# Seven-product block multiplies (Strassen in Winograd's form) in place of eight, with all engine queues written out anew

## Chip, cores and metric

The kernel runs on one core of one Trainium2 chip. The metric is device time in microseconds (us). Before the change the median of 3 runs is 212.93 us (212.54 to 213.19).

## What is computed

```
q = cond @ Wq.T + bq                 # (2, 512), one query row for each batch
k = x @ Wk.T + bk ; v = x @ Wv.T + bv  # x is (2, 2048, 512)
scores = q . k / sqrt(32)            # for each of 16 heads
attn = clip(scores, 0, 1)
out = x + (attn * v) @ Wo.T + bo     # attn scales a head's 32 columns of v
```

All is float32. `k` is never formed: `Wk.T q` is folded once into a small matrix `a`, and the scores are `a . x`. Two large products are left, the values (4096 x 512 by 512 x 512) and the outputs (the same size).

## The kernel before

**Splitting.** A float32 operand is split into `hi`, a rounded copy (float32r), and `lo`, the rest. A product takes three passes: hi by hi, hi by lo, lo by hi (`product`, L208 to L210). The rounded copy is made by ScalarE (ACT), the difference `lo_part` (L424) by VectorE (DVE).

**Tiling.** x stands transposed in SBUF, features on partitions, in 8 chunks of 512 rows, batches in turn. A chunk's values are 4 output tiles by 4 contraction tiles by 3 passes, 48 matmuls of 128x128 weights by 512 columns, into four PSUM banks (`v_bank`); its outputs are 48 more (`o_bank`). With 8 matmuls for the scores (L222, L223) and one that spreads them over partitions (L235) a chunk is 105 matmuls.

**Order.** In `step` TensorE (PE) runs scores and values of chunk c, then the outputs of chunk c-1. DVE adds the bias and multiplies by the clipped scores (`context_tile`, L457), makes `lo`, and adds the output bank, the bias and x (`add_output`, L474). Loops over chunks (`Fori`) hold six of the eight chunks. The last output tile is done in two halves of 256 columns.

**Opening.** x and Wv of the first chunk come in four parts (`first_values`), mixed with the two small chains for `a`: `rows` with Wq (`q_rows`, L276, L279), back to DVE, `rows` with Wk (`a_rows`), back again. Nine bf16 matmuls on zeros (L285) stand ahead. DMAs for x, weights and stores are all issued by SyncE (SP). GpSimd (POOL) clears four tiles and copies `select`.

## Time and profile before

| | |
|---|---|
| median of 3 runs | 212.93 us |
| span of the profiled execution | 211.6 us |
| PE busy | 203.8 us (96%), 895 matmuls |
| DVE busy | 109.0 us (52%), 162 instructions |
| ACT busy | 57.6 us (27%), 85 instructions |
| POOL busy | 3.3 us (2%) |
| HBM read, written | 12.75 MB, 8.39 MB |
| chain that ended last | PE 94%, DMA 3%, DVE 1%, ACT 1% |

The span runs from the first to the last instruction of one execution; the median of the timed runs lies 1.3 us above it. Busy matmul time counts each one's latency, and consecutive matmuls overlap, so their cost is read from one start to the next.

### The profile page before, as it was taken

To read this page: it belongs to the slowest core of one execution; us is meant where nothing else is said; L and a number is where in the kernel's file an instruction comes from. 1 tells how busy PE (TensorE), PEld (TensorE's weight loads), DVE (VectorE), ACT (ScalarE), POOL (GpSimd) and SP (SyncE) were. 2 spreads that over 40 slices of the span, in tenths; PEclk is the share of its full clock that TensorE was granted. 3 is DMA by queue.
4 is the path that set the end of the run, shared out by engine and by line. 5 is a ranking of instruction groups with operands and counts; after the bars stand their busy time and mean duration, and the time that the engine had idled before them with its cause. 6 is when DMAs were issued, how large, how long until landed. Compare 5 with 4: busy or idle time off the path is not lost.

```text
span 211.6 us, 2442 instructions
## 1 busy us (share of the span) xinstructions
PE 203.8 (96%) x895; PEld 166.2 (79%) x895; DVE 109.0 (52%) x162; ACT 57.6 (27%) x85; POOL 3.3 (2%) x9
## 2 busy tenths in 40 slices
PE   7699998999999999999999999999999999999994
PEld 2478766888888888888888888888888888888884
DVE  1567749986344642556344642556344642562222
ACT  3467425660122402250122402250122402220000
POOL 5000000000000000000000000000000000000000
PEclk9999999999999999999999999999999999999999
DMA  4999100155556804000220004000220004000242
GB/s 115 318 283 425 81 3 0 26 201 214 231 198 189 325 9 201 0 0 0 111 87 0 0 0 198 0 0 0 116 82 0 0 0 198 0 0 0 124 177 99
DMA packets 5622, 21.23 MB, mean 100 GB/s; under 512 B 880, under 2 KB 1264, under 8 KB 3696
## 3 DMA queue, kind: packets, MB, share of 16 engines
q1 hardware_dynamic: 5616, 21.14, 27.6%
q8 instruction: 4, 0.07, 0.1%
q14 instruction: 2, 0.02, 0.0%
HBM read 12.75 MB, written 8.39 MB: 100 GB/s over the span
## 4 chain that ended last, share of the span: by engine, by line
PE 94%; DMA 3%; DVE 1%; ACT 1%; issue 0%; SPq 0%; ACTq 0%
PE o_bank L208 14%; PE o_bank L209 14%; PE o_bank L210 14%; PE v_bank L208 12%; PE v_bank L209 12%; PE v_bank L210 12%; PE v_bank L267 6%; PE score_bank L222 3%; PE score_bank L223 3%; DMA x_all<-wv_t 3%; PE score_bank L276 1%; PE score_bank L279 1%; PE score_bank L235 1%; PE o_bank L308 0%; PE o_bank L297 0%; DVE context L457 0%
## 5 line engine op out<-in xcount | busy, mean ns | idle before, releaser
L209 PE MATMUL o_bank<-ctx_lo,wo_hi 128*128 128x512 f32 (+1 forms) x132 | 50.5, 383 | 0.0
L210 PE MATMUL o_bank<-ctx_hi,wo_lo 128*128 128x512 f32 (+1 forms) x132 | 50.5, 383 | 0.0
L208 PE MATMUL o_bank<-ctx_hi,wo_hi 128*128 128x512 f32 (+1 forms) x132 | 50.5, 383 | 0.0
L208 PE MATMUL v_bank<-x_hi,wv_hi 128*128 128x512 f32 x112 | 43.6, 390 | 1.3 <-DVE context L457 1.3
L210 PE MATMUL v_bank<-x_hi,wv_lo 128*128 128x512 f32 x112 | 43.6, 389 | 0.0
L209 PE MATMUL v_bank<-x_lo,wv_hi 128*128 128x512 f32 x112 | 43.6, 389 | 0.0
L474 DVE SCALAR_TENSOR_TENSOR x_all<-o_bank,cols,x_all 128x512 f32 (+1 forms) x31 | 23.3, 750 | 38.4 <-PE o_bank L210 38.4
L457 DVE SCALAR_TENSOR_TENSOR context<-v_bank,cols,attn 128x512 f32<-128x512 f32 x32 | 23.8, 749 | 21.5 <-PE v_bank L210 20.5
L370 ACT CAST ctx_hi<-context 128x512 fp32r<-128x512 f32 x32 | 20.0, 624 | 44.5 <-DVE context L457 44.4
L208 PEld LDWEIGHTS o_bank<-ctx_hi,wo_hi 128*128 128x128 f32 x132 | 24.8, 188 | 4.9
L210 PEld LDWEIGHTS o_bank<-ctx_hi,wo_lo 128*128 128x128 f32 x132 | 24.8, 188 | 4.9
L209 PEld LDWEIGHTS o_bank<-ctx_lo,wo_hi 128*128 128x128 f32 x132 | 24.8, 188 | 4.8
L208 PEld LDWEIGHTS v_bank<-x_hi,wv_hi 128*128 128x128 f32 x112 | 21.0, 188 | 6.0 <-issue 1.7
L210 PEld LDWEIGHTS v_bank<-x_hi,wv_lo 128*128 128x128 f32 x112 | 21.0, 188 | 4.4
L209 PEld LDWEIGHTS v_bank<-x_lo,wv_hi 128*128 128x128 f32 x112 | 21.0, 188 | 4.3
L424 DVE TENSOR_TENSOR ctx_lo<-context,ctx_hi 128x512 fp32r<-128x512 f32 x32 | 21.9, 685 | 0.8
L424 DVE TENSOR_TENSOR x_lo<-x_all,x_hi 128x1024 fp32r<-128x1024 f32 (+1 forms) x18 | 19.8, 1098 | 3.9 <-ACT x_hi L344 3.8
L359 ACT CAST score_hi<-score_bank 128x512 fp32r<-128x512 f32 x8 | 4.7, 588 | 59.3 <-PE score_bank L223 59.3
L353 ACT CAST x_hi<-x_all 128x1024 fp32r (+1 forms) x14 | 14.1, 1047 | 1.8 <-DMA x_all<-x_t 1.7
L222 PE MATMUL score_bank<-x_hi,a_for_hi 128*128 128x512 f32 x32 | 12.5, 389 | 0.0
L223 PE MATMUL score_bank<-x_lo,a_for_lo 128*128 128x512 f32 x32 | 12.5, 389 | 0.0
L442 DVE SCALAR_TENSOR_TENSOR score_parts<-score_hi,const,score_bank 128x512 fp32r<-128x512 f32 x8 | 6.0, 746 | 10.8 <-ACT score_hi L359 10.8
(61 smaller groups left out, 102.9 us busy)
## 6 DMA issues: line engine op xcount, KB each, us to landing
x_all<-x_t SPq DMA_DIRECT2D x7, 1024.0 KB, 4.9
out_t<-x_all SPq DMA_DIRECT2D x7, 1024.0 KB, 3.9
x_all<-x_t SPq DMA_DIRECT2D x4, 256.0 KB, 6.2
x_all<-wv_t SPq DMA_DIRECT2D x4, 256.0 KB, 6.9
x_all<-wq_t SPq DMA_DIRECT2D x4, 256.0 KB, 6.3
x_all<-wk_t SPq DMA_DIRECT2D x4, 256.0 KB, 8.3
x_all<-wo_t SPq DMA_DIRECT2D x1, 1024.0 KB, 10.7
out_t<-x_all SPq DMA_DIRECT2D x3, 256.0 KB, 2.5
```

The costliest lines, as they stand in the source:

```text
L208: pe.matmul(out, w_hi, y_hi, start=first, stop=False)
L209: pe.matmul(out, w_hi, y_lo, start=False, stop=False)
L210: return pe.matmul(out, w_lo, y_hi, start=False, stop=last)
L222: pe.matmul(bank, a_for_hi[:, b, k, :], x_hi[:, b, k, :], start=k == 0, stop=False)
L223: mm = pe.matmul(bank, a_for_lo[:, b, k, :], x_lo[:, b, k, :], start=False, stop=k == KT - 1)
L267: mm = pe.matmul(v_bank[m][:, :], w[:, k, m * P:(m + 1) * P], y[:, 0, k, :], start=k == 0 and kind == 0, stop=last)
L353: nc.scalar.copy(x_hi[:, b, first:first + KT // 2, :].rearrange("p k n -> p (k n)"), x_chunk(c, first, KT // 2)).then_inc(x_hi_ready, 1)
L370: nc.scalar.copy(ctx_hi[:, b, m, :], context[:, m, :]).then_inc(ctx_hi_ready, 1)
L424: return nc.vector.tensor_tensor(to, of, hi.bitcast(F32), ALU.subtract)
L442: nc.vector.scalar_tensor_tensor(out=score_parts[:, :], in0=score_hi[:, :].bitcast(F32), scalar=const[:, C_LO:C_LO + 1], in1=score_bank[b] ...
L457: nc.vector.scalar_tensor_tensor(out=context[:, m, :], in0=v_bank[m][:, :], scalar=bv[:, m:m + 1], in1=attn[:, :], op0=ALU.add, op1=ALU.mu ...
L474: nc.vector.scalar_tensor_tensor(out=x_tile, in0=o_bank[n % 2][:, :], scalar=bo[:, n:n + 1], in1=x_tile, op0=ALU.add, op1=ALU.add).then_in ...
```

## The change

The rows are grouped in four supers of 1024. In a super, x transposed is a 2 x 2 matrix of blocks of 256 features by 512 rows, and Wv and Wo are 2 x 2 matrices of 256 x 256 blocks. A block product is 2 output tiles by 2 contraction tiles by 3 passes, 12 matmuls. There are eight such matrices, called phases (V0, V1, O0, V2, O1, V3, O2, O3: values or outputs of a super). V0 is done with the eight plain block products; the other seven phases take seven products, with sums of blocks.

- DVE forms the sums of x blocks (`x_t1` to `x_t4`), of context blocks (`context_t1` to `t4`) and of weight blocks (`wv_sum`, `wo_sum`); seven operands of 1024 columns per phase are rounded by ACT (`hi`) and have `lo` made by DVE.
- Three result blocks are kept running in PSUM: ACT copies the bank out with bias and sign (`copy_out`), PE adds the next product to the same bank, DVE adds a second bank to the copy (`add_out`).
- The clip and the product of scores and values are one DVE instruction of 1024 columns (`context`).
- x of supers 0 to 2 is added to the outputs by an accumulating DMA issued by POOL; the last super's x by DVE.
- The first loads are x's first half rows beside blocks W11 and W21; Wq comes ahead of x's right half. PE's loops are written out. The nine first matmuls read a constant and wait for no DVE instruction.
- The last output is stored as two parts of 512 columns.

The core of the diff (empty lines left out):

```diff
+B11, B21, T2, T1, T3, T4, B22 = range(7)
+W11, W12, S2, S1, S3, W22, S4 = range(7)
+W21 = S3
+Q11, Q12, Q21, Q22 = range(4)
+FIRST_PHASE_KINDS = (B11, B21, T3, B22)
+VALUES, OUTPUTS = "values", "outputs"
+PHASES = ((VALUES, 0), (VALUES, 1), (OUTPUTS, 0), (VALUES, 2), (OUTPUTS, 1), (VALUES, 3), (OUTPUTS, 2), (OUTPUTS, 3))
+LAST = len(PHASES) - 1
+VALUES_AT = [PHASES.index((VALUES, s)) for s in range(SUPERS)]
+OUTPUTS_AT = [PHASES.index((OUTPUTS, s)) for s in range(SUPERS)]
+def made(kind, phase):
+    return phase + (kind in FIRST_PHASE_KINDS)
...
+            def store(s, q):
+                sp.wait_ge(residual_added[q], 16 * (s + 1))
+                sp.dma_start(out_t[s, q], output_set(s)[:, q, :]).then_inc(stored[q], 16)
...
+            for k in range(2):
+                sp.dma_start(work[1][:, k, :], first_t[k]).then_inc(first_loaded[k], 16)
+            sp.dma_start(x_raw[:, Q11, :], wv_t).then_inc(first_loaded[2], 16)
+            load_x(0, Q21)
+            sp.dma_start(const[:, :], constants).then_inc(small_loaded, 16)
+            for h in range(2):
+                sp.dma_start(work[0][:, (Q12, Q22)[h], :], wq_t[:, h, :]).then_inc(wq_loaded[h], 16)
+            load_x(0, Q12)
+            load_x(0, Q22)
+            for h in range(2):
+                sp.dma_start(wo_sums[:, h, :], wk_t[:, h, :]).then_inc(wk_loaded[h], 16)
+            sp.dma_start(wo_raw.rearrange("p t n -> p (t n)"), wo_t.rearrange("p b n -> p (b n)")).then_inc(wo_loaded, 16)
+            next_x(1)
...
+            def product(phase, kind, form, bank, grows=False):
+                what, s = PHASES[phase]
+                operand_ready(kind, phase)
+                w_hi, w_lo = (wv_hi, wv_lo) if what == VALUES else (wo_hi, wo_lo)
+                if what == VALUES and phase == 1:
+                    pe.wait_ge(wv_hi_ready[form], wv_count(form))
+                    pe.wait_ge(wv_lo_ready[form], wv_count(form))
+                if what == OUTPUTS and s == 0:
+                    pe.wait_ge(wo_hi_ready[form], 1)
+                    pe.wait_ge(wo_lo_ready[form], 1)
+                for j in range(2):
+                    at = slice(j * P, (j + 1) * P)
+                    for k in range(2):
+                        hi, lo = w_hi[:, form, k, at], w_lo[:, form, k, at]
+                        pe.matmul(bank[:, j, :], hi, form_hi[:, kind, k, :], start=k == 0 and not grows, stop=False,
+                                  skip_group_check=grows)
+                        pe.matmul(bank[:, j, :], hi, form_lo[:, kind, k, :], start=False, stop=False,
+                                  skip_group_check=grows)
+                        mm = pe.matmul(bank[:, j, :], lo, form_hi[:, kind, k, :], start=False, stop=k == 1,
+                                       skip_group_check=grows)
+                    mm.then_inc(done[kind], 1)
+            def product_b11(phase):
+                if phase == 1:
+                    pe.wait_ge(first_out[Q21], 2)
+                wait(pe, out11_added, phase - 1)
+                product(phase, B11, W11, grown(phase))
+            def product_b21(phase):
+                if phase == 1:
+                    pe.wait_ge(first_out[Q22], 2)
+                wait(pe, out21_copied, 2 * (phase - 1))
+                product(phase, B21, W12, side(phase))
+            def product_t2(phase):
+                pe.wait_ge(b11_copied, 2 * phase)
+                product(phase, T2, S2, grown(phase), grows=True)
+            def product_t1(phase):
+                if phase == 1:
+                    pe.wait_ge(first_out[Q12], 2)
+                wait(pe, out12_added, phase - 1)
+                product(phase, T1, S1, last_bank)
+            def product_t3(phase):
+                pe.wait_ge(u2_copied, 2 * phase)
+                product(phase, T3, S3, grown(phase), grows=True)
+            def product_t4(phase):
+                pe.wait_ge(u3_copied, 2 * phase)
+                product(phase, T4, W22, grown(phase), grows=True)
+            def product_b22(phase):
+                pe.wait_ge(out22_added, phase)
+                product(phase, B22, S4, last_bank, grows=True)
...
+            def opening_products():
+                for k in range(2):
+                    for bank, form in ((banks[0], W11), (banks[1], W21)):
+                        for w, y in ((wv_hi, form_hi), (wv_lo, form_hi), (wv_hi, form_lo)):
+                            pe.wait_ge((wv_lo_ready if w is wv_lo else wv_hi_ready)[form], k + 1)
+                            if k == 0:
+                                pe.wait_ge(first_half_lo if y is form_lo else first_half_hi, 1)
+                            else:
+                                pe.wait_ge((lo_ready if y is form_lo else hi_ready)[B11], 1)
+                            for j in range(2):
+                                pe.matmul(bank[:, j, :], w[:, form, k, j * P:(j + 1) * P], y[:, B11, k, :],
+                                          start=k == 0 and w is wv_hi and y is form_hi, stop=False)
...
+            opening_products()
+            first_product(banks[0], W12, B21, False, True)
+            first_product(banks[1], W22, B21, False, True)
...
+            for phase in range(2, LAST):
+                what, s = PHASES[phase]
+                before, s_before = PHASES[phase - 1]
+                product_b11(phase)
+                if phase == 2:
+                    spread(1, 0)
+                product_t4(phase - 1)
+                product_b22(phase - 1)
+                if before == VALUES:
+                    scores(s_before, 1).then_inc(score_done, 1)
+                product_b21(phase)
+                if what == VALUES:
+                    if s == 2:
+                        pe.wait_ge(a_ready, 6)
+                    scores(s, 0).then_inc(score_done, 1)
+                product_t2(phase)
+                if before == VALUES:
+                    spread(s_before, 1)
+                product_t1(phase)
+                if what == VALUES:
+                    spread(s, 0)
+                product_t3(phase)
+            product_b11(LAST)
+            product_t4(LAST - 1)
+            product_b22(LAST - 1)
+            product_t2(LAST)
+            product_b21(LAST)
+            product_t3(LAST)
+            product_t1(LAST)
+            product_t4(LAST)
+            product_b22(LAST)
...
+            def hi(kind, phase):
+                what, s = PHASES[phase]
+                if what == VALUES:
+                    semaphore, count = {
+                        B11: (x_loaded[Q11], loads(Q11, s)), B21: (x_loaded[Q21], loads(Q21, s)),
+                        B22: (x_loaded[Q22], loads(Q22, s)),
+                        T1: (x_t1_ready, s), T2: (x_t2_ready, s), T3: (x_t3_ready, s), T4: (x_t4_ready, s)}[kind]
+                    act.wait_ge(semaphore, count)
+                else:
+                    semaphore = {B11: context_ready[Q11], B21: context_ready[Q21], B22: context_ready[Q22],
+                                 T1: c_t1_ready, T2: c_t2_ready, T3: c_t3_ready, T4: c_t4_ready}[kind]
+                    act.wait_ge(semaphore, s + 1)
+                before, s_before = PHASES[phase - 1]
+                if phase == 1 and kind in (T1, T2):
+                    act.wait_ge(a_rows_done, 1)
+                elif before == VALUES and kind in FIRST_PHASE_KINDS:
+                    act.wait_ge(score_done, score_number(s_before, kind in (T3, B22)) + 1)
+                else:
+                    wait(act, done[kind], 2 * (phase - 1))
+                nc.scalar.copy(flat(form_hi, kind), raw(kind, phase)).then_inc(hi_ready[kind], 1)
...
+            def copy_out(phase, q, of, scale, semaphore, done_semaphore, done_count):
+                what, s = PHASES[phase]
+                bias = bv if what == VALUES else bo
+                home_free(phase, q)
+                for j in range(2):
+                    act.wait_ge(done_semaphore, done_count + j + 1)
+                    tile = 2 * (q in (Q21, Q22)) + j
+                    nc.scalar.activation(result_set(phase)[:, q, j * ROWS:(j + 1) * ROWS], of[:, j, :], ACT.Identity,
+                                         bias=bias[:, tile:tile + 1], scale=scale).then_inc(semaphore, 1)
+            def copy_b11(phase):
+                copy_out(phase, Q11, grown(phase), 1.0, b11_copied, done[B11], 2 * (phase - 1))
+            def copy_u2(phase):
+                copy_out(phase, Q12, grown(phase), -1.0, u2_copied, done[T2], 2 * (phase - 1))
+            def copy_u3(phase):
+                copy_out(phase, Q22, grown(phase), -1.0, u3_copied, done[T3], 2 * (phase - 1))
+            def copy_out21(phase):
+                copy_out(phase, Q21, grown(phase), 1.0, out21_copied, done[T4], 2 * (phase - 1))
...
+            def add_residual(s, q, semaphore, count):
+                pool.wait_ge(semaphore, count)
+                pool.dma_start(output_set(s)[:, q, :], x_t[s, q], accum_op=ALU.add).then_inc(residual_added[q], 16)
...
+            for s in range(3):
+                at = OUTPUTS_AT[s]
+                add_residual(s, Q11, out11_added, at)
+                add_residual(s, Q22, out22_added, at)
+                add_residual(s, Q21, out21_copied, 2 * at)
+                add_residual(s, Q12, out12_added, at)
...
+            def context(s, q):
+                half = q in (Q12, Q22)
+                phase = VALUES_AT[s]
+                semaphore, count = {Q11: (out11_added, phase), Q21: (out21_copied, 2 * phase),
+                                    Q12: (out12_added, phase), Q22: (out22_added, phase)}[q]
+                if s == 0:
+                    semaphore, count = first_out[q], 2
+                dve.wait_ge(semaphore, count)
+                dve.wait_ge(relu_ready, score_number(s, half) + 1)
                 nc.vector.scalar_tensor_tensor(
...
+            def add_out(phase, q, bank, kind, copied, semaphore):
+                dve.wait_ge(done[kind], 2 * phase)
+                dve.wait_ge(copied, 2 * phase)
+                if phase == LAST:
+                    dve.wait_ge(x_added[q], 1)
+                to = pair(result_set(phase), q)
+                nc.vector.tensor_tensor(to, bank[:, :, :], to, ALU.add).then_inc(semaphore, 1)
...
+            def context_t1(phase):
+                s = PHASES[phase][1]
+                dve.wait_ge(hi_ready[B11], made(B11, phase))
+                dve.wait_ge(context_ready[Q11], s + 1)
+                dve.wait_ge(context_ready[Q12], s + 1)
+                blocks = context_set(s)
+                nc.vector.tensor_tensor(blocks[:, Q11, :], blocks[:, Q11, :], blocks[:, Q12, :], ALU.add).then_inc(c_t1_ready, 1)
...
+            first_w_hi(W11, 0)
+            first_w_part(W11, 0)
+            first_half(0, first_half_hi, first_half_lo)
+            first_w_part(W21, 0)
+            first_w_hi(W11, 1)
+            first_w_part(W11, 1)
+            first_half(1, hi_ready[B11], lo_ready[B11])
+            first_w_part(W21, 1)
+            wv_part(W12)
+            wv_part(W22)
+            wv_sum(0)
+            first_lo(B21, Q21)
+            split_cond()
+            wv_sum(1)
+            wq_part(0)
+            wq_part(1)
+            wv_sum(2)
+            wq_part(2)
+            wq_part(3)
+            first_lo(T3, Q12)
+            wv_sum_part(S1, 0)
+            first_lo(B22, Q22)
+            wv_sum_part(S2, 1)
+            wv_sum(3)
+            wv_sum_part(S4, 2)
+            wk_part(0)
+            wk_part(1)
+            wk_part(2)
+            wk_part(3)
+            wo_sum(0)
+            scale_q()
+            x_t1(1)
+            scale_bk()
+            x_t3(1)
+            wo_part(W11, 0)
+            wo_part(W12, 1)
+            wo_sum(1)
+            lo(T1, 1)
+            x_t2(1)
+            wo_sum(2)
+            fill_a()
+            split_a(0)
+            sum_c()
+            wv_sum_part(S3, 3)
+            lo(T2, 1)
+            x_t4(1)
+            wo_sum_part(S2, 1)
+            wo_sum(3)
+            wo_sum_part(S1, 0)
+            lo(B11, 1)
+            lo(B21, 1)
             split_scores(0, 0)
+            lo(T4, 1)
+            lo(T3, 1)
+            wo_sum_part(S3, 2)
+            lo(B22, 1)
+            split_scores(0, 1)
+            wo_part(W22, 3)
+            context(0, Q11)
+            context(0, Q21)
+            add_out11(1)
+            context(0, Q12)
+            context(0, Q22)
+            wo_sum_part(S4, 3)
+            lo(B11, 2)
...
```

## Rows read from the trace of the kernel before

**Rows 1.** The page: busy time by engine, and two of the 40-slice rows.
```profile
PE 203.8 (96%) x895; PEld 166.2 (79%) x895; DVE 109.0 (52%) x162; ACT 57.6 (27%) x85; POOL 3.3 (2%) x9
DVE  1567749986344642556344642556344642562222
PEclk9999999999999999999999999999999999999999
```
**Rows 2.** Waits: engine, line, releaser; us in total, times, longest.
```profile
DVE x_all L474 <- PE o_bank L210: 38.4, 31, 2.0
DVE context L457 <- PE v_bank L210: 20.5, 18, 1.4
```
**Rows 3.** Timeline of PE's last outputs: start us, us, engine, line, operation.
```profile
198.73 0.39 PE L210 MATMUL o_bank<-ctx_hi,wo_lo 128*128 128x512 f32 x1
...
205.53 0.39 PE L210 MATMUL o_bank<-ctx_hi,wo_lo 128*128 128x512 f32 x1
```
**Rows 4.** Timeline of the opening: PE, and ACT's first rounding of weights.
```profile
1.46 4.02 PE L285 MATMUL o_bank<-context 128*128 128x512 bf16 x9 [1.46 <-DVE context L478]
6.80 0.62 ACT L346 CAST wv_hi<-x_all 128x512 fp32r<-128x512 f32 x1 [1.62 <-DMA x_all<-wv_t]
7.56 2.04 PE L267 MATMUL v_bank<-x_hi,wv_hi 128*128 128x512 f32 x4 [2.08 <-ACT wv_hi L346]
12.82 1.23 PE L267 MATMUL v_bank<-x_hi,wv_hi 128*128 128x512 f32 x4
32.70 0.47 PE L208 MATMUL v_bank<-x_hi,wv_hi 128*128 128x512 f32 x1 [1.27 <-DVE context L457]
```
**Rows 5.** Timeline: back-to-back instructions of DVE and ACT.
```profile
22.07 0.68 DVE L424 TENSOR_TENSOR wv_lo<-x_all,wv_hi 128x512 fp32r<-128x512 f32 x1
22.67 1.22 DVE L424 TENSOR_TENSOR x_lo<-x_all,x_hi 128x1024 fp32r<-128x1024 f32 x1
...
25.99 1.22 DVE L424 TENSOR_TENSOR x_lo<-x_all,x_hi 128x1024 fp32r<-128x1024 f32 x1
27.12 0.28 DVE L521 CAST a_for_hi<-o_bank 128x128 fp32r<-128x128 f32 x1
...
34.50 0.74 DVE L457 SCALAR_TENSOR_TENSOR context<-v_bank,cols,attn 128x512 f32<-128x512 f32 x1
35.16 0.68 DVE L424 TENSOR_TENSOR ctx_lo<-context,ctx_hi 128x512 fp32r<-128x512 f32 x1
...
69.24 1.99 ACT L353 CAST x_hi<-x_all 128x1024 fp32r x2
```
**Rows 6.** Groups by shape: busy us, mean ns; idle before.
```profile
L424 DVE TENSOR_TENSOR x_lo<-x_all,x_hi 128x1024 fp32r<-128x1024 f32 x14 | 17.0, 1215 | 0.0
L442 DVE SCALAR_TENSOR_TENSOR score_parts<-score_hi,const,score_bank 128x512 fp32r<-128x512 f32 x8 | 6.0, 746 | 10.8 <-ACT score_hi L359 10.8
L353 ACT CAST x_hi<-x_all 128x1024 fp32r x12 | 12.0, 1046 | 0.1
L364 ACT ACTIVATE relu<-score_bank,c_score 128x512 f32<-128x512 f32 x8 | 5.5, 689 | 15.7 <-PE score_bank L235 15.7
```
**Rows 7.** Windows: busy us of PE, PEld, DVE, ACT, POOL; PEclk, DMA share, GB/s.
```profile
0.00:8.00 8.00, 4.46 (x10) 1.66 (x11) 1.73 (x3) 3.04 (x4) 2.97 (x8) 1.00 0.64 168
8.00:14.00 6.00, 6.00 (x17) 4.66 (x17) 4.86 (x10) 3.81 (x7) 0.29 (x1) 1.00 0.96 290
14.00:22.00 8.00, 7.86 (x39) 6.29 (x38) 5.13 (x12) 5.18 (x9) 0.00 (x0) 1.00 1.01 405
```
**Rows 8.** DMA issues: count, KB each, median us from issue to landing.
```profile
out_t<-x_all SPq DMA_DIRECT2D x7, 1024.0 KB, 3.9
out_t<-x_all SPq DMA_DIRECT2D x3, 256.0 KB, 2.5
out_t<-x_all SPq DMA_DIRECT2D x2, 128.0 KB, 1.9
```
**Rows 9.** Timeline of the end: the last matmul and the last DVE instruction.
```profile
208.51 0.28 PE L210 MATMUL o_bank<-ctx_hi,wo_lo 128*128 128x256 f32 x1
208.83 0.48 DVE L562 SCALAR_TENSOR_TENSOR x_all<-o_bank,cols,x_all 128x256 f32<-128x256 f32 x1 [0.95 <-PE o_bank L210]
```

More of the change, by code:

```diff
@@ new lines, in _ @@
+            load_x(0, Q12)
[4 more added lines that the diff above has]
+            next_x(1)
+            next_x(2)
+            store(0, Q11)
+            store(0, Q22)
+            next_x(3)
+            store(0, Q21)
+            store(0, Q12)
+            store(1, Q11)
@@ L204, in _ @@
+            for q, count in ((Q11, SUPERS), (Q22, SUPERS), (Q21, SUPERS + 1), (Q12, SUPERS + 1)):
+                sp.wait_ge(stored[q], 16 * count)
         @block.tensor
         def _(pe):
-            def product(out, w_hi, w_lo, y_hi, y_lo, first, last):
-                pe.matmul(out, w_hi, y_hi, start=first, stop=False)
-                pe.matmul(out, w_hi, y_lo, start=False, stop=False)
-                return pe.matmul(out, w_lo, y_hi, start=False, stop=last)
-            def value_tile(b, m, k):
-                at = slice(m * P, (m + 1) * P)
-                return product(v_bank[m][:, :], wv_hi[:, k, at], wv_lo[:, k, at],
-                               x_hi[:, b, k, :], x_lo[:, b, k, :], k == 0, k == KT - 1)
@@ L272, in rows, with operand_ready @@
[L272 to L279 removed]
+            def operand_ready(kind, phase):
+                pe.wait_ge(hi_ready[kind], made(kind, phase))
+                pe.wait_ge(lo_ready[kind], made(kind, phase))
@@ new lines, in _ @@
+            context_t4(2)
+            split_scores(1, 1)
+            lo(T3, 2)
+            add_out11(2)
+            lo(T4, 2)
+            lo(B22, 2)
+            x_t1(3)
+            lo(B21, 3)
+            split_a(1)
+            x_t3(3)
+            lo(T1, 3)
+            x_t2(3)
+            add_out22(2)
+            lo(T2, 3)
+            lo(T3, 3)
+            context(1, Q11)
+            x_t4(3)
+            context(1, Q12)
+            add_out12(2)
+            lo(T4, 3)
+            add_out11(3)
@@ new lines, in _ @@
+            lo(B22, 3)
+            split_scores(2, 0)
+            lo(B11, 4)
+            context_t1(4)
+            context(1, Q21)
+            context(1, Q22)
+            lo(B21, 4)
+            lo(T1, 4)
+            context_t2(4)
+            add_out22(3)
+            lo(T2, 4)
+            context_t3(4)
+            lo(B11, 5)
+            context_t4(4)
+            x_t1(5)
+            add_out12(3)
+            lo(T4, 4)
+            split_scores(2, 1)
+            lo(T3, 4)
+            add_out11(4)
@@ new lines, in _ @@
+            lo(B22, 4)
+            lo(B21, 5)
+            x_t3(5)
+            context(2, Q11)
+            context(2, Q12)
+            lo(T1, 5)
+            x_t2(5)
+            add_out22(4)
+            lo(T3, 5)
+            lo(T2, 5)
+            x_t4(5)
+            context(2, Q21)
+            context(2, Q22)
+            lo(T4, 5)
+            add_out12(4)
+            lo(B22, 5)
+            add_out11(5)
+            lo(B11, 6)
+            split_scores(3, 0)
+            context_t1(6)
@@ new lines, in _ @@
+            lo(B21, 6)
+            context_t3(6)
+            lo(T1, 6)
+            context_t2(6)
+            add_out22(5)
+            lo(T2, 6)
+            context(3, Q11)
+            context_t4(6)
+            lo(B11, 7)
+            context(3, Q21)
+            add_out12(5)
+            lo(T4, 6)
+            split_scores(3, 1)
+            lo(T3, 6)
+            add_out11(6)
+            lo(B22, 6)
+            lo(B21, 7)
+            context(3, Q12)
+            context_t1(7)
+            context(3, Q22)
@@ new lines, in _, with constant_columns @@
+            lo(T1, 7)
+            context_t2(7)
+            add_out22(6)
+            lo(T2, 7)
+            context_t3(7)
+            context_t4(7)
+            lo(T3, 7)
+            add_x(Q11)
+            add_out12(6)
+            lo(T4, 7)
+            lo(B22, 7)
+            add_x(Q12)
+            add_out11(7)
+            add_x(Q22)
+            add_out22(7)
+            last_out21(0)
+            last_out21(1)
+            last_out12(0)
+            last_out12(1)
+def constant_columns(cond, columns):
```

956 lines of the change are left out of this document (596 added, 360 removed).

## Prediction

> **What bounds the kernel now.** I read the page's busy shares first: PE 96%, DVE 52%, ACT 27%, the granted TensorE clock full in every slice, which is the 2.4 GHz level [rows 1]. The chain of waits is 94% PE, and the waits say the same from the other side: DVE stands 38.4 us and 20.5 us before its two commonest instructions because PE is not done [rows 2]. So PE is the bound, and DVE and ACT are covered by it. What a matmul costs is not its 389 ns of latency but the step to the next start: from 198.73 to 205.53 there are 30 steps, 0.2267 us each [rows 3]. Outside that stream PE loses time in the opening: it stands 2.08 us before 7.56, its first 12 matmuls then take until 12.82 (0.44 us each, although the granted clock reads 1.00 there), and it stands again 1.27 us before 32.70 [rows 4, 7].
>
> **What is removed from PE.** Seven of eight phases drop one block product of 12 matmuls: 84 x 0.2267 = 19.0 us, all of it on the path. Scores, spreads, the chains for `a` and the nine first matmuls keep their counts. The last tile loses its 24 half-width matmuls, about 0.12 us each, for 12 full ones: 2.9 less 2.7, another 0.2 us. The Trainium skill's page "TensorE: Matmul & The Clock Gate", section "Back-to-back issue gap", gives an isolated 512-column matmul N/2.4 + 2.5 = 216 ns and a sustained stream about 131 ns. By the first the 84 would be worth 18.1 us, by the second 11.0; the stream here runs at 227, so the row decides.
>
> **What is added to DVE, and whether PE still covers it.** DVE is in order, so its load is counted in steps from one start to the next. A 1024-column subtraction with both inputs in SBUF costs 1.13 us (25.99 to 27.12), a 512-column one 0.60 (22.07 to 22.67), a 512-column one from PSUM 0.66 (34.50 to 35.16) [rows 5]. Counting the written-out list after the change:
> - 1024 columns, SBUF: 52 `lo`, 12 x sums, 16 context sums, 16 `context`, 3 `add_x`: 99 x 1.13 = 111.9 us. `context` is a fused instruction that before only ran from PSUM; I take 1.13, its upper bound is two halves, 1.32.
> - 1024 columns from PSUM: 20 `add_out`. No row has the size; the bounds are 1.13 and 2 x 0.66 = 1.32, I take 1.25: 25.0 us.
> - 512 columns: 31 x 0.60 + 12 x 0.66 = 26.5 us; six of 256 columns 2 us; the small ones of the chains 3.3 us.
>
> Together 169 us. PE after the change has 684 + 64 + 8 + 16 = 772 matmuls at 0.2267 = 175.0 us, 2.5 us for the slow first 12 and 1.9 us for 18 small ones: 179.4 us. DVE goes from half idle to 94% of PE's own time. It stays under PE in sum, but the margin is 10 us in the whole kernel, and the order decides. (The Trainium skill's page "VectorE: DVE Perf Modes", section on the TRN2 errata, counts 58 cycles plus columns from SBUF and 120 from PSUM. The rows agree at 512, and for `add_out` it gives 1.19 us, an estimate that would take 1.2 us from DVE's sum and nothing from PE's.)
>
> ACT gets 52 roundings at 0.94 (two in 1.99, the second adding 0.94 [rows 5]), 62 copies of 512 columns from PSUM at 0.6 to 0.69 [rows 6], 16 score steps and some 30 weight parts: about 110 to 120 us, two thirds of PE. It bounds nothing in sum; its copies matter because `product_t3` and `product_t4` wait for them. One block product (12 x 0.2267 = 2.72 us) stands between. The second half of a copy needs about 0.4 us until the bank is done and 0.69 for itself, and may stand behind a rounding of 1.05: 2.1 us, so it fits with 0.6 us to spare.
>
> **The opening, walked.** The DMAs brought 1.34 MB by 8 us, 3.1 MB by 14, 6.3 MB by 22 [rows 7]. The first load is now 512 KB holding x and both weight blocks; Wv's first 256 KB was there at 6.80 as the second transfer [rows 4]. I take 6.5 for the new first load (bounds 5.5 and 7.5) and PE's start at 7.3, one rounding later. 48 matmuls with 12 slow ones end at 20.6; Wq (3.2 MB down the queue) is there by 14 to 15 and is no stall. Its 8 matmuls end at 22.5. Now the copy of `q_rows` stands on ACT behind three parts of Wk, which may not start before those 8 are done: 3 x 0.55 + 0.6, so it is ready at 25.2, covered by 12 matmuls to 25.2. DVE can't go past `wk_part` before ACT, so it reaches `scale_q` at 27.0; Wk's 8 matmuls end at 30.7, and their last copy behind `hi(T1, 1)` at 32.7, covered by the next 12 (33.4). From `scale_q` DVE's list is solid work. Its prefix sums give `split_a(0)` 36.6, `lo(B11, 1)` 42.5, `split_scores(0, 1)` 49.1, `lo(B11, 2)` 57.2. PE wants these at 37.2, 43.5, 49.2 and 56.7. So at 57.3 PE has done 198 matmuls, with about 0.6 us of stall. Before, the 198th would end at 32.70 + 117 x 0.2267 = 59.2 (81 were done by 32.70): 1.9 us gained. After this PE's supply grows: DVE has 15 to 23 us a phase against 19 to 23 on PE. I walk the same sums to the end of V3: `lo(B11, 4)` at 94.5 against 100.1, `lo(B11, 6)` at 136.4 against 142.5. PE is the bound again.
>
> **The end.** The last DVE instruction grows from 256 to 512 columns (0.48 to 0.75 [rows 6, 9]) and its store from 128 to 256 KB (1.9 to 2.5 us [rows 8]): 0.9 us added. The larger stores before it lie beside the last products.
>
> **Other edits, at nothing.** The residual by POOL's accumulating DMAs has 20 us or more before its buffer is reused; no row shows such a DMA, the nearest is a 1 MB store of 3.9 us [rows 8]. Above 8 us each it would reach the end (a rival below), and since it replaces a DVE input it can't gain. SP now waits in list order for x reloads; the first reload is free at about 21 us and needed at 28. The first nine matmuls start earlier but end before the data, gaining nothing.
>
> **Sum**, against the profiled execution: 211.6 - 19.0 - 0.2 - 1.9 + 0.9 = 191.4 us. For hand-offs that don't fit I add one wait of the size seen at 32.70, 1.3 us, giving 192.7. What lies around the span is 1.3 us: 194.0 us.
>
> **Rivals.**
> 1. DVE binds through the first four phases. For it: no slack at four milestones before 57 us. If the fused and PSUM instructions take their upper bounds and each cross-engine wait costs 0.1 us, the 29 us of list from `scale_q` grow by 3 us, and O0, V2 by 3 more: 197 to 204, say 200. Against it: back-to-back rows show no such cost. 22%.
> 2. Slower than before: the engines fall into step. The in-order DVE stands at each `add_out` until its product is done, as it now does for 38.4 us [rows 2], with the next products' `lo` behind it. The price is up to one product, 2.72 us, at one place in each of seven phases: 19 us, 213 with the end, and 215 or more if ACT's copies add a second such place. It turns the sign from 2.9 us a phase on. Against it: the order puts `lo` ahead of the adds. 6%.
> 3. Accumulating DMAs are slow. SP's last four stores stand behind the store of super 2's Q12, which waits for the twelfth one. It starts about 15 us before PE ends; its price begins where it takes over 12 us, 196 to 202. The Trainium skill's page "SBUF — State Buffer", section "Who interferes with whom", says that GpSimd is shut out of the shared port while DVE runs certain instructions, which would delay its descriptors; no run here shows it yet. 3%.
> 4. The change doesn't do what it says: PE's step doesn't hold. After a stand of 2 us the first 12 matmuls took 2.5 us extra [rows 4]; two or three such stands make 199 to 202. 3%.
>
> **How the numbers follow.** The forecast (PE bound, under 4 us lost) has 66% and by itself spans 190.5 to 197. The low end takes no lost hand-off, a first load at 5.5 us and a full cover; the high end reaches into rival 1 up to 201. About 8 in 10 lie between. A measurement here can tell about 0.3%, 0.6 us. Faster: cases 1, 3, 4 and the forecast, 94%; within 0.3%: 1%; slower: most of rival 2, 5%.
>
> **What would show it.** Right: PE's count falls by 84 + 12 to about 799, its step stays 0.227, DVE's busy share goes to about 90%, the waits for DVE on PE shrink to under 20 us, O2 and O3 take 19.1 us each. The opening is right if the 198th full matmul ends near 57 us. It is wrong in the first load if PE starts after 8 us, in the DVE prices if `add_out` or `context` step over 1.3 us, in the hand-offs if PE waits on `copy_out` by more than 0.5 us a phase. If PE waits for `lo` after 100 us, rival 1 or 2 holds.

## The result and the profile after

The changed kernel takes 189.62 us (median of 6 runs, 189.01 to 190.35) against 213.06 us before: the ratio is 0.8905, 95% interval 0.8872 to 0.8939. The forecast was 194.0 us with a range of 190.5 to 201. The sign and most of the size were right; the time lies 0.9 us below the range.

The page of the changed kernel: busy time by engine, DVE and PE in 40 slices, the granted clock.

```profile
span 188.3 us, 2351 instructions
PE 182.8 (97%) x799; PEld 148.0 (79%) x799; DVE 168.8 (90%) x184; ACT 115.6 (61%) x158; POOL 14.7 (8%) x21
PE   8999999899999999999999999999999999999993
DVE  1799979999999999999899999998897899799752
PEclk9999999999999999999999999999999999999999
```

Against [rows 1], PE has 96 fewer matmuls, and DVE goes from 52% to 90%, within 0.2 us of the 169 us that the prediction counted. Who PE waited for (line, releaser: us in total, times, longest):

```profile
PE bank_z L433 <- PEq L1311: 0.8, 1, 0.8
PE score_bank L387 <- DVE c_score L1044: 0.6, 1, 0.6
PE bank_x L328 <- issue: 0.4, 1, 0.4
PE bank_x L402 <- DVE form_lo L820: 0.3, 1, 0.3
PE score_bank L448 <- ACT relu L649: 0.2, 1, 0.2
```

After 55 us there is no wait at all. The timeline at its three marks: the first real matmul, the 199th (the first with `wo_hi`), the last, and the add behind it.

```profile
3.94 0.62 ACT L641 CAST form_hi<-work 128x512 fp32r<-128x512 f32 x1 [1.92 <-DMA work<-first_t]
4.70 1.00 PE L420 MATMUL bank_x<-form_hi,wv_hi 128*128 128x512 f32 x2
5.53 0.63 PE L420 MATMUL bank_x<-form_hi,wv_lo 128*128 128x512 f32 x2
...
10.53 1.09 PE L402 MATMUL bank_x<-form_hi,wv_hi 128*128 128x512 f32 x4
...
54.73 0.47 PE L328 MATMUL bank_x<-form_hi,wo_hi 128*128 128x512 f32 x1 [0.40 <-issue]
...
184.71 0.39 PE L332 MATMUL bank_z<-form_hi,wo_lo 128*128 128x512 f32 x1
185.13 0.69 DVE L950 TENSOR_TENSOR work<-bank_z,work 128x512 f32<-128x512 f32 x1 [0.67 <-PE bank_z L332]
```

From 54.73 to 184.71 are 573 steps in 129.98 us: 0.2268 us each, the step of [rows 3], with nothing lost in 130 us. The distance to the predicted span (192.7 by the sum, 188.3 measured) therefore has three parts: PE reached the 199th matmul at 54.7, not 57.3 (2.6 us); the hand-off wait of 1.3 us that I had added isn't there; and from the start of the last matmul to the end there are 3.6 us, where the prediction's terms give 4.0 (the 3.1 us of [rows 9] and 0.9 added). That is 4.3 of the 4.4 us.

### The profile page after: what moved, and what is told of

It reads as the page before. It is cut to its first block, busy times and chain, and to the rows that moved or that the text cites. A ratio compares the mean times of both kernels' runs of the same rounds, so it can differ in the third digit from the quotient of the medians.

```text
span 188.3 us, 2351 instructions
## 1 busy us (share of the span) xinstructions
PE 182.8 (97%) x799; PEld 148.0 (79%) x799; DVE 168.8 (90%) x184; ACT 115.6 (61%) x158; POOL 14.7 (8%) x21
## 4 chain that ended last, share of the span: by engine, by line
PE 80%; DVE 9%; DMA 7%; issue 2%; SPq 1%; ACT 0%; DVEq 0%
PE bank_y L328 9%; PE bank_y L332 9%; PE bank_y L330 9%; PE bank_x L328 8%; PE bank_x L332 8%; PE bank_x L330 8%; PE bank_z L332 7%; PE bank_z L328 7%; PE bank_z L330 7%; PE score_bank L387 4%; PE score_bank L388 4%; DVE form_lo L820 4%; DMA x_raw<-wv_t 3%; DMA x_raw<-x_t 3%; DVE work L1058 1%
## 5 line engine op out<-in xcount | busy, mean ns | idle before, releaser
L820 DVE TENSOR_TENSOR form_lo<-work,form_hi 128x1024 fp32r<-128x1024 f32 (+1 forms) x38 | 40.3, 1079 | 4.6 <-ACT form_hi L544 4.6
L544 ACT CAST form_hi<-work 128x1024 fp32r<-128x1024 f32 x28 | 29.0, 1051 | 24.5 <-PE score_bank L388 13.2
L579 ACT ACTIVATE work<-bank_y,const 128x512 f32<-128x512 f32 x30 | 20.0, 688 | 10.2 <-PE bank_y L332 10.2
L328 PE MATMUL bank_x<-form_hi,wo_hi 128*128 128x512 f32 x52 | 20.3, 391 | 0.4 <-issue 0.4
L330 PE MATMUL bank_x<-form_lo,wo_hi 128*128 128x512 f32 x52 | 20.3, 390 | 0.0
L332 PE MATMUL bank_x<-form_hi,wo_lo 128*128 128x512 f32 x52 | 20.3, 390 | 0.0
L579 ACT ACTIVATE work<-bank_x,const 128x512 f32<-128x512 f32 x24 | 16.3, 687 | 6.4 <-PE bank_x L332 6.3
L844 DVE SCALAR_TENSOR_TENSOR work<-relu,work 128x1024 f32<-128x1024 f32 x16 | 19.1, 1218 | 0.0
L330 PE MATMUL bank_y<-form_lo,wv_hi 128*128 128x512 f32 x48 | 18.7, 390 | 0.0
L328 PE MATMUL bank_y<-form_hi,wv_hi 128*128 128x512 f32 x48 | 18.7, 390 | 0.0
L332 PE MATMUL bank_y<-form_hi,wv_lo 128*128 128x512 f32 x48 | 18.7, 390 | 0.0
L820 DVE TENSOR_TENSOR form_lo<-x_raw,form_hi 128x1024 fp32r<-128x1024 f32 x15 | 18.2, 1217 | 0.0
```

The lines of the kernel that those rows point to most:

```text
L328: pe.matmul(bank[:, j, :], hi, form_hi[:, kind, k, :], start=k == 0 and not grows, stop=False, skip_group_check=grows)
L330: pe.matmul(bank[:, j, :], hi, form_lo[:, kind, k, :], start=False, stop=False, skip_group_check=grows)
L332: mm = pe.matmul(bank[:, j, :], lo, form_hi[:, kind, k, :], start=False, stop=k == 1, skip_group_check=grows)
L544: nc.scalar.copy(flat(form_hi, kind), raw(kind, phase)).then_inc(hi_ready[kind], 1)
L579: nc.scalar.activation(result_set(phase)[:, q, j * ROWS:(j + 1) * ROWS], of[:, j, :], ACT.Identity, bias=bias[:, tile:tile + 1], scale=sca ...
L820: return nc.vector.tensor_tensor(to, of, hi.bitcast(F32), ALU.subtract)
```

## Experiments

### Is PE alone the bound, or PE and DVE together?

`dup_b11` does the product of B11 twice in each of the seven phases, with the same result; it puts the eighth product's cost back on PE and adds nothing to DVE or ACT.

```diff
-                    for k in range(2):
+                    for k in range(4 if twice else 2):
+                        k = k % 2
...
-                product(phase, B11, W11, grown(phase))
+                product(phase, B11, W11, grown(phase), twice=True)
```

> The changed kernel with the product of B11 by W11 done twice in each of the seven phases of seven products (12 more matmuls, same result): the eighth product put back on PE alone. Theory A (PE is the bound in every phase): 7 x 12 x 0.2267 = 19.0 us more, 208.6 us. Theory B (DVE is as much the bound as PE): where DVE has no slack the added matmuls are hidden; phase 1 hides 0 to 2.7 us, so 16 to 19 us more; if DVE bound through phase 3, only 11 us more, 201 us.

It took 208.68 us (ratio to the kernel before 0.9821, 0.9769 to 0.9872): 19.1 us above the changed kernel's 189.6. The window from the 199th matmul to the last start:

```profile
55.78:202.10 146.32, 146.32 (x647) 121.18 (x646) 120.70 (x111) 78.98 (x101) 10.50 (x12) 1.00 0.45 115
```

The same window of the changed kernel:

```profile
54.73:184.71 129.98, 129.98 (x574) 107.73 (x574) 120.16 (x111) 77.46 (x101) 10.50 (x12) 1.00 0.49 130
```

In both, PE's busy time fills the window. The difference, 16.34 us, is 72 x 0.227 = 16.3 us: in phases 2 to 7 each removed matmul is worth its full step. The 12 added in phase 1 moved the 199th matmul by only 1.05 us (55.78 against 54.73) where their steps are 2.7. Of the missing 1.7 us, 1.0 is chance: in this execution a load of x landed earlier and the DVE instruction behind it, `x_t3(1)`, started at 26.20 instead of 27.16. From that instruction's start to the 199th matmul it is 29.58 us against 27.57, so the 12 matmuls cost 2.0 us and the other 0.7 was room that PE had: its waits of 0.6 and 0.4 us in the opening shrink to 0.16 and none. The profiled spans differ by 17.4 us, the medians by 19.1; the profiled execution of `dup_b11` is the shortest of its five (207.51), that of the changed kernel the second longest of its six (190.13). So nearly all of the 84 matmuls is paid for, and the small part that isn't lies in the opening.

### Who sets the opening

`warm0` leaves out the nine first bf16 matmuls.

```diff
-WARM_UP = 9
+WARM_UP = 0
```

> The changed kernel without its nine first bf16 matmuls. Theory A (the nine matmuls, which end at 4.77 us where the first real one starts at 4.70, are what keeps the first twelve real ones at 0.227 us a step): the first twelve step at 0.43 us again, 2.5 us more on PE by the 24th matmul. From 27 us on DVE's list, not PE, sets the 198th matmul, so at the end 0 to 1.5 us of it are left: 189.6 to 191.1 us. Theory B (the slow steps of the kernel before came from late loads, not from PE having stood): steps stay 0.227 and the time stays 189.6.

The time was 189.98 us (189.39 to 190.07), no change that can be told. The trace shows both halves of theory A:

```profile
4.76 1.19 PE L420 MATMUL bank_x<-form_hi,wv_hi 128*128 128x512 f32 x2 [4.76 <-ACT form_hi L641]
5.75 1.05 PE L420 MATMUL bank_x<-form_hi,wv_lo 128*128 128x512 f32 x2
6.61 1.05 PE L420 MATMUL bank_x<-form_lo,wv_hi 128*128 128x512 f32 x2
...
12.68 1.07 PE L402 MATMUL bank_x<-form_hi,wv_hi 128*128 128x512 f32 x4
```

Having stood, PE steps at 0.43 us (the granted clock of 4.7 to 10 us reads 1.00 all the same), and the 25th matmul starts at 12.68 where it was 10.53: 2.15 us late. But the 199th starts at 54.66 (54.73 in the changed kernel). All of it is absorbed, so something else sets that point. Part of it goes where DVE waits for x before `x_t3(1)`: it reaches that point later and stands 0.44 us there in place of 1.15.

`dve_early` puts two more DVE instructions of 1024 columns (a constant less itself, into a spare tile) behind `x_t3(1)` and `x_t4(1)`.

```diff
             x_t3(1)
+            extra()
...
             x_t4(1)
+            extra()
```

> Two more DVE instructions of 1024 columns (2.3 us) in the opening, behind x_t3 and x_t4 of phase 1. Theory A (DVE's list sets the 198th matmul): all of it reaches the end, 189.6 + 2.3 = 191.9 us. Theory B (DVE has slack there): 189.6 to 190.3.

It took 191.82 us (191.51 to 192.22), 2.2 above the changed kernel, and its 199th matmul started at 56.70, 2.0 us later. The two DVE instructions cost 2 x 1.13 = 2.3, so DVE's list passes nearly all of it on.

The load of x before `x_t3(1)` lands at a different time in each execution, and that gives a second reading of the same thing. The start of `x_t3(1)`, that of the 199th matmul and the time between, in us:

| run | `x_t3(1)` | 199th | between |
|---|---|---|---|
| changed kernel | 27.16 | 54.73 | 27.57 |
| its copy (`after_again`, below) | 27.07 | 54.63 | 27.56 |
| `warm0` | 27.09 | 54.66 | 27.57 |
| `split_first` (below) | 28.30 | 55.87 | 27.57 |
| `dve_phases` (below) | 28.39 | 55.96 | 27.57 |
| `hoist` (below) | 26.54 | 54.12 | 27.58 |
| `dve_early` | 26.86 | 56.70 | 29.84 |
| `dup_b11` | 26.20 | 55.78 | 29.58 |

In the six runs whose opening has the same work from there on, PE's 199th matmul follows the DVE instruction by the same time to 0.02 us, over a range of 1.9 us of its start. In `dve_early` the distance grows by 2.27 us, the full cost of the two instructions. From `x_t3(1)` on, the opening is DVE's, and its start is set by that load.

`swap_wo` adds nothing; it puts two `lo` parts of Wo, long ready, ahead of `x_t3(1)`, before which DVE stood 1.15 us for a load of x.

```diff
-            x_t3(1)
             wo_part(W11, 0)
             wo_part(W12, 1)
+            x_t3(1)
```

> The changed kernel with two lo parts of Wo (0.60 us each, ready) ahead of x_t3 of phase 1, before which DVE stands 1.15 us for a load. Theory A (DVE's list from scale_q at 23.5 to the lo before the 198th matmul at 54.5 sets PE's time): DVE gains up to 1.15 us, PE's waits of 0.6 us at 34.38 and 0.4 us at 54.73 go: 188.6 to 189.0 us. Theory B (PE is the bound there too and its waits are incidental): no change, 189.6.

188.71 us (187.89 to 190.28). Since the effect is near the scatter, it ran again in the same rounds as the changed kernel (`after_again`, an unchanged copy).

> The changed kernel itself once more, as the measure for the two beside it: 189.6 us, span 188.3, the third phase's first product (the 199th matmul) starting at 54.7 us, within 1 us as the load of x before x_t3 lands.

> The kernel with two lo parts of Wo ahead of x_t3, again, now beside the changed kernel in the same rounds. If DVE's list sets the opening, it is 0.9 to 1.6 us below the changed kernel: 188.0 to 188.7 us. If its 188.7 of the first time was chance, it is equal to it within 0.3 us.

`after_again` took 189.35 us (ratio 0.8908, 0.8859 to 0.8956), `swap_wo_again` 188.66 us (0.8878, 0.8835 to 0.8921). The intervals overlap, but both times the medians fall by 0.7 to 0.9 us, and of the 144 pairs that the 12 executions with the swap make with the 12 without, the swap is the faster in 116. Both pairs of profiles give a span 1.6 us shorter; the profiled executions of the changed kernel are among its slower ones, so the medians are the fairer size. In the changed kernel's copy and in the swapped one, DVE at `x_t3` (L912):

```profile
27.07 1.23 DVE L912 TENSOR_TENSOR x_raw<-x_raw 128x1024 f32<-128x1024 f32 x1 [1.20 <-DMA x_raw<-x_t]
```

```profile
25.50 1.29 DVE L820 TENSOR_TENSOR wo_lo<-work,wo_hi 128x512 fp32r<-128x512 f32 x2
26.71 1.22 DVE L912 TENSOR_TENSOR x_raw<-x_raw 128x1024 f32<-128x1024 f32 x1
```

The wait is gone and the 199th matmul starts at 53.06 in place of 54.63, 1.6 us earlier, which the trace carries to the end (span 186.6 against 188.2). Beside the 1.20 us, 0.18 us of another wait for x is missing in this execution, which the swap didn't cause. PE's waits are then 0.7 us for the first data and 0.4 us before the 199th matmul: PE and DVE are nearly level in the opening.

### The loads and the slow first steps

`split_first` cuts the two first loads of 512 KB into four of 256 KB, with rows half as long. The waits on them count 32 in place of 16.

```diff
-                sp.dma_start(work[1][:, k, :], first_t[k]).then_inc(first_loaded[k], 16)
+                for a in (0, ROWS):
+                    sp.dma_start(work[1][:, k, a:a + ROWS], first_t[k, :, a:a + ROWS]).then_inc(first_loaded[k], 16)
```

> The two 512 KB first loads cut into four of 256 KB (x half, weight half), rows of 2 KB in place of 4 KB. Theory A (longer rows and fewer transfers brought the first data at 3.94 us instead of the 6.5 I had assumed): PE starts 0.5 to 2 us later and, since over 2 us of standing brings the slow steps back, up to 2.5 us more is lost on PE early; at the end 0.5 to 2 us. Theory B (the first transfer always lands near 4 us and only what stands behind it matters): PE starts within 0.3 us of 4.70, end time within 0.5 us.

It took 190.72 us (189.57 to 191.57), about 1.1 us more by the medians, with ranges that overlap. Its timeline:

```profile
4.31 0.62 ACT L642 CAST form_hi<-work 128x512 fp32r<-128x512 f32 x1 [2.29 <-DMA work<-first_t]
7.86 0.62 ACT L642 CAST form_hi<-work 128x512 fp32r<-128x512 f32 x1 [2.63 <-DMA work<-first_t]
```

The same 512 KB were complete at 4.31 us; in the ten profiles with uncut loads they were there at 3.94 to 4.35. The second 512 KB came at 7.86, the uncut ones at 5.16 to 5.79. So the first pair is as early as before and theory B holds for PE's start (5.07, against 4.70 to 5.11), while the second pair is some 2 to 2.7 us late, as theory A has it. DVE comes to the wait before `x_t3(1)` at 27.25, where it is there at 25.7 to 26.7 in the others without the swap; the 199th matmul starts 1.1 us later than in the changed kernel (55.87), which is inside what the load of x moves it by from run to run. Whether row length or the number of transfers delays the second pair was not separated. Nor does the cut explain the 6.80 us at which the kernel before had its first weights [rows 4]: they were the second of its pieces of 256 KB, and here two such pieces were there by 4.31. What delayed them there stays open.

`before_warm14` bridges the stand of 2.08 us in the kernel before with 14 first matmuls instead of 9.

```diff
-WARM_UP = 9
+WARM_UP = 14
```

> The kernel before with 14 first bf16 matmuls in place of 9, so that they end near 7.6 us, where its first real matmul starts at 7.56. Theory A (standing 2.08 us is what made the first twelve slow): the twelve step at 0.227 us, 2.5 us gained by the 12th; if PE stays the bound, 210.5 us. If the loads or the chains for a then stop it (x part 2 and Wv part 2 came at 12.96 and 14.98), the gain is eaten: 212 to 213. Theory B: the twelve stay slow and nothing changes.

The 12 slow steps of [rows 4] go: with the start at 7.04, the 13th matmul starts at 9.99, 0.246 us a step.

```profile
7.04 1.28 PE L267 MATMUL v_bank<-x_hi,wv_hi 128*128 128x512 f32 x4
...
9.99 1.07 PE L267 MATMUL v_bank<-x_hi,wv_hi 128*128 128x512 f32 x4
...
18.45 1.05 PE L297 MATMUL o_bank<-const,q_rows 128*128 128x2 f32 x8 [0.99 <-ACT q_rows L383]
20.68 2.07 PE L276 MATMUL score_bank<-ctx_hi,q_parts 128*128 128x512 f32 x4 [0.15 <-DVE q_parts L424]
33.41 0.47 PE L208 MATMUL v_bank<-x_hi,wv_hi 128*128 128x512 f32 x1 [1.25 <-DVE context L457]
```

The time is 213.14 us, ratio 1.0008 (0.9974 to 1.0042): the gain is eaten. PE now waits for Wv's third part (0.64 us) and for `q_rows` (0.99), and after that has eight matmuls at the slow step again (2.07 and 1.80 us for four). Here the granted clock shows them: it is 0.53 from 20.6 to 24.2 us, nearly all of it the lower level of 1.2 GHz. But they are not what eats the gain: three of the ten executions have a mean granted clock of 0.998 or more, so hardly such a stretch, and take 211.03, 212.07 and 212.43 us, and the eleven such executions of the kernel before have a median of 212.22. The first slow steps are real in both kernels, and in neither does their absence move the end by an amount that can be told.

### How much room DVE has after the opening

`dve_phases` adds two instructions of 1024 columns in each of phases 2 to 6, 11.3 us in all, behind `lo(B21, p)` and `lo(T2, p)`.

```diff
             lo(B21, 2)
+            extra()
...
             lo(T2, 2)
+            extra()
```

> Two more DVE instructions of 1024 columns in each of phases 2 to 6, 11.3 us in all, none in the opening. My forecast had DVE about 1.2 us a phase lighter than PE and 5 us ahead by the fourth phase: 10 x 1.13 less 5 x 1.2 less 5 leaves 0 to 2 us, 189.6 to 191.6 us. Rival 1 (DVE has no margin in the early phases): each phase passes on 2.3 us less 1.2, 5 us more, 194 to 195 us or above.

It took 194.98 us (193.34 to 195.81). Its profiled run had a later load of x in the opening (DVE stood 2.29 us before `x_t3`), and its 199th matmul started at 55.96, 1.2 us late. From there:

```profile
55.96:190.40 134.44, 131.83 (x574) 107.17 (x574) 131.07 (x121) 76.13 (x101) 10.51 (x12) 1.00 0.47 124
```

134.44 less 129.98 is 4.5 us of the 11.3, so DVE had about 7 us of room in the five phases. The expectation that followed from my forecast, 0 to 2 us more, missed, and the time is the one that I had put beside rival 1 (194 to 195). PE's waits say where the room ends:

```profile
PE bank_z L330 <- DVE work L857: 2.4, 3, 0.9
```

These three waits (0.82 us at 83.81, 0.66 at 106.17, 0.91 at 128.46) stand before the last product of phases 2, 3 and 4, which adds to the bank that `add_out22` (L857 here) has to read first. Counted there, the loss is 1.0, 1.3, 1.2, 0.6 and 0.4 us in phases 2 to 6. My rule took the lead of about 5 us that the `lo` of the next products have; the add has less. In the changed kernel it ends 2.1 us before PE needs the bank in phases 2 and 3 (79.50 against 81.58, 100.55 against 102.66), less than half of the 5 us that I counted with.

### Is the order worth anything? Rival 2 tried

`hoist` moves one DVE instruction in each of four phases: `add_out22(p)`, p from 2 to 5, four places forward. Nothing is added.

```diff
+            add_out22(2)
             split_a(1)
             x_t3(3)
             lo(T1, 3)
             x_t2(3)
-            add_out22(2)
```

> The add of the second block row (it waits for the third product chained into the bank) moved four instructions forward on DVE in phases 2 to 5, so that DVE stands there until PE is done, with the next products' lo parts behind it. Rival 2 (engines fall into step): DVE stands 2 to 4 us a phase, PE stands for a lo after it, 4 to 10 us more, 194 to 200 us. Forecast's view (DVE is 5 us ahead of what PE needs): 189.6 to 191 us.

It took 201.23 us (198.79 to 201.43), 11.6 us more, above the 194 to 200 that I had put beside rival 2. Some of the longest waits of DVE, ACT and PE, in us in total, times, longest:

```profile
DVE work L855 <- ACT work L579: 13.6, 4, 5.0
ACT form_hi L544 <- DVE work L890: 11.2, 2, 5.9
ACT form_hi L544 <- DVE x_sum L920: 7.3, 3, 5.0
```

```profile
PE bank_x L328 <- ACT work L579: 3.7, 3, 1.9
PE bank_y L328 <- ACT work L579: 2.3, 1, 2.3
```

and two windows, the second of which holds the wait of 2.27 us:

```profile
76.00:98.00 22.00, 20.74 (x92) 16.83 (x91) 19.50 (x20) 10.49 (x14) 2.60 (x3) 1.00 0.71 180
98.00:120.00 22.00, 19.73 (x81) 15.88 (x80) 18.46 (x17) 13.55 (x19) 0.86 (x1) 0.92 0.21 79
```

From the 199th matmul to the last it needs 141.7 us for 130.0, 2.9 us for each moved instruction. That this is near the price that rival 2 put on one lost product (2.72 us) is partly chance, for it is made of two things. DVE stands at the add, the sums and `lo` of the next products stand behind it, ACT's roundings behind those, and ACT's copies, for which PE waits, behind the roundings: all three queues are in order. PE's idle time is 6.8 us (the window's length less PE's busy 134.9). Beside it PE's busy time grows by 4.9 us, most of it because after its two longest stands, of 2.27 and 1.89 us, some 15 steps take 0.43 us:

```profile
110.59 0.79 PE L328 MATMUL bank_y<-form_hi,wo_hi 128*128 128x512 f32 x1 [2.27 <-ACT work L579]
111.18 0.63 PE L330 MATMUL bank_y<-form_lo,wo_hi 128*128 128x512 f32 x1
111.61 0.63 PE L332 MATMUL bank_y<-form_hi,wo_lo 128*128 128x512 f32 x1
```

The granted clock shows it: 0.92 over the 22 us, 0.79 from 108 to 116 us and 0.81 from 130 to 139, behind the second stand, against 1.00 in the rest; part of both stretches is at the lower level of 1.2 GHz. After the wait of 1.26 us before 85.11 the steps stayed 0.23. The one of the four executions whose mean granted clock is 0.997 takes 198.79 us, the three at 0.982 to 0.983 take 201.21 to 201.43, so, by that one execution, the slow steps are worth about 2.4 us and the waits the other 9 or so. The Trainium skill's page "TensorE: Matmul & The Clock Gate", section "HAM oscillation — how this bites in real kernels", says that waits inside the stream make the clock fall back. This run agrees, with waits shorter than those of the page's own case.

### The end

`swap_store2` is `swap_wo` with the last add and store of 512 columns cut in two of 256.

```diff
             last_out12(1)
+            last_out12(2)
```

(`last_out12(1)` and `(2)` take 256 columns each, and SP stores each behind it.)

> As swap_wo, and the last add and store of 512 columns cut in two of 256, so that the last store is 128 KB. By my rows of before the smaller store lands 0.5 us sooner and the second add ends 0.1 us later: 0.4 us less than swap_wo. If landing time is fixed by anything but size, no difference.

188.46 us (187.68 to 188.71), ratio 0.8860 (0.8818 to 0.8902), against 188.66 beside it; the profiled spans are 186.7 and 186.6. No difference that can be told. The 256 KB stores of the changed kernel land in 2.0 us, not the 2.5 of [rows 8], so there was less to take. Cutting the last product itself into halves was not tried.

## Why the prediction was right and where it was wrong

**84 matmuls less, 19.0 us, all on the path: right.** The step is 0.2268 us, and putting the product back costs 16.3 us in six phases, exactly its steps; in phase 1 it costs 2.0 of 2.7.

**DVE nearly full but not the bound in steady state: right.** 168.8 us busy against 169 counted. The two can be compared because I counted steps and the page merges overlapping instructions. `context` and `add_out`, the two priced by bounds, both measured 1.22 us long, and follow one another at 1.13 (from 47.03 on, two in 2.35), the lowest value of both bounds. For the adds from PSUM I had taken 1.25, 2.4 us too much over 20; small parts that I didn't trace made up for it, so the agreement to 0.2 us is partly luck. The 1.19 us that the prediction worked out by the Trainium skill's page "VectorE: DVE Perf Modes", section on the TRN2 errata, was nearer than mine and still above the row of 1.13. What the sum hid is where the margin is thin: I walked the `lo` and not the adds, and `dve_phases` shows that `add_out22` has 2.1 us to spare, not 5.

**The first load at 6.5 us (bounds 5.5 to 7.5): wrong, the main error.** It landed at 3.94. I carried the 6.80 of [rows 4], the time of the second piece of 256 KB in the kernel before, over to the first load of the changed one. `split_first` shows that two pieces of 256 KB can be there by 4.31 as well, so their size doesn't explain it; why they were late in the kernel before stays open. The lower bound should have been the first rounding in the kernel before, which its trace has at 4.56 us. How much of the 2.6 us at the 199th matmul this term alone is worth was not tested: `split_first` delayed the second 512 KB by over 2 us, and that matmul started 1.1 us later.

**12 slow steps, 2.5 us: wrong.** They came in the kernel before behind the stand between 5.48 and 7.56, and `before_warm14`, which fills it, is without them. With the load at 3.94 the nine first matmuls (until 4.77) meet the first real one, and only the first pair is slow. I had written that they end before the data and gain nothing. `warm0` brings the slow steps back and shows that, with the data that early, they do not reach the end.

**The walk of the opening: the mechanism was right, its dates were late.** PE was 4.0 us ahead of my walk at the Wq rows (16.57 against 20.6) and 2.6 ahead at the 199th matmul: the rest was lost to DVE's list and to x's load before `x_t3`, which I had as ready. The steps from `scale_q` on were right: the prediction has 30.2 us from its start to the end of `lo(B11, 2)`, the trace 31.0 (23.53 to 54.51), of which 1.15 is that load. `dve_early` and `swap_wo` show from both sides that this list sets the 199th matmul, and so does the constant 27.57 us behind `x_t3(1)`.

**A hand-off wait of 1.3 us: wrong, there is none.** The second half of a copy fits under the product between, as the walk had said (0.6 us to spare); the allowance had no row behind it. This (1.3 us) and the tail, 0.4 us shorter than I had counted (3.6 us from the last matmul's start to the end, for 4.0: the last store landed in 2.0 us, not 2.5), make the other 1.7 us of the difference.

**The rivals.** Rival 1, DVE the bound until the fourth phase, is right for the opening alone. Its price was not paid; DVE's costs came at their lower bounds, which fits, but no run shows what the upper ones would have done. `dve_phases` shows how near it was: three more instructions of 1024 columns ahead of `add_out22(2)` cost PE 1.0 us. Rival 2 did not happen, but `hoist` shows that it was one ordering decision away: four moved instructions give back half of the whole gain. Rival 3: the prediction gives two limits that disagree, 8 and 12 us; the 12 accumulating loads take a median of 5.3 us and at most 8.4, and the last one only kept SP from the store of Q11 until 178.7 us, 2 us after that block was ready, which no one waited for. Rival 4's mechanism, slow steps after PE has stood, occurs in `warm0`, `hoist` and `before_warm14`; in the changed kernel only the first pair is slow.

**The range.** The low end took a first load at 5.5 us together with no lost hand-off. With the load's true lower bound of 4 us in it, the range would have begun near 189. Two allowances for the unknown had been put on the same side.

## What to carry to other kernels

Taking a product away pays its full issue time only while the vector engines keep up, and a sum of busy times doesn't tell that: walk the in-order lists to every point where PE needs something, the adds that free a bank as well as the next operands, since four instructions in the wrong place cost about as much here as four products. In an opening, look which list sets the first steady phase before improving another: removing 2 us of slow matmuls gained nothing that can be told in two kernels, and moving two ready instructions ahead of one that waits for a load gained 0.7 to 0.9 us by the medians, 1.6 in the profiled pairs. For when a first load lands, take the earliest landing that the trace shows as one bound, not only the one that the code waited for.

## What was unexpected of the hardware

- A DVE instruction of 1024 columns is followed by the next after 1.13 us whether one input is in PSUM or all are in SBUF (85.17 to 86.30 in the changed kernel, an add from PSUM). The same holds for a plain add of 512 columns: 691 ns long from PSUM (L950), 686 from SBUF (L820). The 0.66 against 0.60 of [rows 5], from which the prediction took its price for PSUM, sets a fused instruction from PSUM beside a plain one from SBUF.
- Two loads of 512 KB with rows of 4 KB were both there by 5.16 to 5.79 us (ten profiles); the same bytes as four loads of 256 KB, in the one profile there is, only by 7.86.
- From `x_t3(1)` to the 199th matmul six executions agree to 0.02 us, while the start of `x_t3(1)` behind its load moves by 1.9 us from one to another.
- PE's steps were 0.43 us behind stands of 1.89 and 2.27 us in `hoist`, and 0.23 behind one of 1.26. In the openings of `warm0` and of the kernel before the granted clock reads 1.00 over steps of 0.43 us.
- Accumulating DMAs of 512 KB from POOL took 5.3 us to land (median; at most 8.4), with DVE 90% busy; POOL's own issue took 0.87 us each.
